# Cross attention computed transposed: row maxima turned to the keys' side, column-tiled weighing, sums inverted by ScalarE, keys and values made in the routing stage

## What is computed

```python
x = x + einsum('bsd,sod->bso', layernorm(x), ctx[itok])       # one of 32 matrices per position
x = x + routed_ffn(layernorm(x))                               # 8 experts, 256 -> 512 -> 256, gelu
q, k, v = proj(layernorm(x), Wq, bq), proj(ctx, Wk, bk), proj(ctx, Wv, bv)   # 16 heads of 16
scores = einsum('bhqd,bhkd->bhqk', q, k) / 4 + mask * -1e9
x = x + einsum('bsd,ed->bse', heads(softmax(scores) @ v), Wo) + bo
x = x + nvfp4_ffn(layernorm(x))                                # fake-quantised, 256 -> 1024 -> 256
```

## Time and profile before

| what | us |
|---|---|
| three runs | 759.76, 760.28, 765.82 |
| median | 760.28 |
| span of the profiled execution | 786.0 |
| TensorE busy in it | 611.1 (78%) |
| VectorE busy | 583.2 (74%) |
| ScalarE busy | 404.4 (51%) |
| GpSimd busy | 209.1 (27%) |

### The profile page before, as it was taken

The page is one execution under the profiler, slowest core; times in us unless marked ns, Lnnn a source line. Parts: engine busy times, 40 slices in busy tenths (PEclk is TensorE's granted clock), DMA queues, the critical chain, the costliest instruction groups (busy, mean ns, idle before and its releaser), DMA issues.

```text
span 786.0 us, 14622 instructions
## 1 busy us (share of the span) xinstructions
PE 611.1 (78%) x4239; PEld 484.1 (62%) x4240; DVE 583.2 (74%) x1515; ACT 404.4 (51%) x780; POOL 209.1 (27%) x254
## 2 busy tenths in 40 slices
PE   5496786609899999958999999999744666766766
PEld 3384655409899898847888888887611433344424
DVE  6274666855645665667888889888648999999997
ACT  1341323003434233336565667665785798778762
POOL 5617363424644565510112222211100000000000
PEclk9698797858999999978999999999975799987998
DMA  8763242259375667261000000000000000000001
GB/s 321 228 209 118 71 137 76 96 181 385 107 232 173 185 197 230 78 185 34 1 0 0 0 0 0 0 1 1 2 3 1 0 27 27 13 27 13 27 27 54
DMA packets 35230, 68.22 MB, mean 87 GB/s; under 512 B 5405, under 2 KB 24238, under 8 KB 34160
## 3 DMA queue, kind: packets, MB, share of 16 engines
q1 hardware_dynamic: 28512, 52.20, 20.2%
q0 software_dynamic: 5520, 13.61, 5.1%
q10 hardware_dynamic: 1152, 1.88, 0.8%
HBM read 53.62 MB, written 15.80 MB: 88 GB/s over the span
## 4 chain that ended last, share of the span: by engine, by line
PE 36%; DVE 19%; issue 15%; ACT 13%; DMA 7%; another core or an unknown queue 3%; SPq 3%; POOL 2%; DVEq 1%; ACTq 0%; POOLq 0%
PE bank L1289 5%; PE quad L1162 4%; PE quad L1114 4%; PE quad L1273 3%; PE bank L1304 3%; PE bank L1171 3%; ACT hqT L1013 2%; DMA x_after_ffn<-row,niU 2%; PE quad L1454 2%; PE quad L1463 2%; ACT ctxs L996 2%; PE quad L1264 2%; DVE hh L2200 2%; DMA early<-in_W 2%
## 5 line engine op out<-in xcount | busy, mean ns | idle before, releaser
L746 ACT ACTIVATE hid<-quad,early 128x128 f32<-128x128 f32 x156 | 44.5, 368 | 87.8 <-PE quad L1162 86.5
L1162 PE MATMUL quad<-xts,early 128*128 128x128 f32 x624 | 76.5, 283 | 4.5 <-DMA early<-in_W 4.3
L1162 PEld LDWEIGHTS quad<-xts,early 128*128 128x128 f32 x624 | 74.9, 199 | 6.6 <-issue 5.5
L1171 PE MATMUL bank<-W2s,hid 128*128 x312 | 70.5, 379 | 0.0
L624 POOL TENSOR_TENSOR X<-fo,X 128x256 f32<-128x256 f32 (+1 forms) x32 | 21.8, 682 | 178.0 <-DVE fo L2046 178.0
L1289 PE MATMUL bank<-nVB,nPT 128*128 128x34 f32 x512 | 63.0, 279 | 0.0
L1171 PEld LDWEIGHTS bank<-W2s,hid 128*128 128x128 f32 x312 | 57.7, 190 | 7.1
L1289 PEld LDWEIGHTS bank<-nVB,nPT 128*128 128x128 f32 x512 | 59.6, 191 | 3.7
L1489 PE MATMUL bank<-dT,hqT 128*128 128x256 bf16 x224 | 41.0, 348 | 25.8 <-ACT hqT L1013 25.7
L577 POOL DMA_INDIRECT x_after_ffn<-row,niU x39 | 39.0, 1000 | 58.9 <-DVE row L1804 41.9
L1799 DVE SCALAR_TENSOR_TENSOR row<-bank,sco,row 128x256 f32<-128x256 f32 x39 | 18.5, 474 | 47.2 <-PE bank L1171 44.3
(11 more groups left out here) (325 smaller groups left out, 1431.6 us busy)
## 6 DMA issues: line engine op xcount, KB each, us to landing
early<-in_W SPq DMA_DIRECT2D x37, 514.0 KB
row<-rows_by_expert SPq DMA_DIRECT2D x38, 134.0 KB
early<-in_ctxO SPq DMA_DIRECT2D x4, 1024.0 KB, 7.8
ctxs<-in_ctxT SPq DMA_DIRECT2D x4, 1024.0 KB
W2s<-in_W SPq DMA_DIRECT2D x8, 512.0 KB
X<-x_after_ffn SPq DMA_DIRECT2D x7, 516.0 KB, 7.2
out<-yo SPq DMA_DIRECT2D x14, 256.0 KB, 2.1
early<-in_W ACTq DMA_DIRECT2D x2, 514.0 KB
```

Of the source, the lines that this page charges most:

```text
L746: ins = act.activation(hid[:, u, c * P:(c + 1) * P], bank[2 + u][:, c * P:(c + 1) * P], ACT.Gelu, bias=W1r[:, k, DC * H2 + c:DC * H2 + c + 1])
L1162: ins = pe.matmul(bank[2 + u][:, n * P:(n + 1) * P], W1r[:, m % RING, c * H2 + n * P:c * H2 + (n + 1) * P], xt[:, u, c, :], start=c == 0, ...
L1171: ins = pe.matmul(bank[6 + u % 2][:, 0:D], hid[:, u, c * P:(c + 1) * P], W2s[:, bass.ds(ex, 1), c, :].rearrange("p o s -> p (o s)"), start ...
```

## The change

**Keys and values early.** They leave the attention. In the routing stage, behind `ranks(g-1)` of groups 1 to 8, TensorE computes keys and values of the pair g-1 straight from `ctxs`, and ScalarE copies them to `Kall` and `Vall`, which hold all pairs. Wk, Wv and bk are loaded ahead of the other weights for it, with a semaphore of their own. SP waits for VectorE's first logits (`s_dl`) before it loads the last FFN's weights.

**Scores twice.** `score` now begins with a product of ones and the mask in bf16 and adds the raw products to it in PSUM. VectorE takes only the maxima of these out (`row_max`, one instruction a half), divides them into three bf16 parts (`maxima`, four small instructions for both halves), TensorE turns them (`maxima_turn`), ScalarE copies them (`maxima_out`). `score_turned` then computes the scores with keys on partitions: a product of a selecting matrix of -1 and the maxima, and on top of it keys times queries; no probabilities are turned any more. Each of the two steps has 8 heads and all 256 queries. `exps` reads them from PSUM, with the mask of the key as its bias, and writes the probabilities in the form in which the weighing needs them. Both kinds of scores use the same four banks, in halves.

**Weighing and sums.** `weigh` has the values of two heads (32 columns) as the weight and streams 256 queries of the probabilities; four such products go to four column strips of TensorE, and four more with ones as weight give the sums, repeated on the same partitions as the values. ScalarE inverts the sums of a whole batch by a logarithm and an exponential with scale -1 (`inverse_sums`), in a table set that it loads once, VectorE multiplies (`divide`, one 128x512 instruction a batch). The result has channels on partitions, so `project` uses it without a turn. `add_rows` of VectorE adds the product straight to the residual stream, to which GpSimd has added the bias before (`biased`); GpSimd spreads the keys (`keys_in`).

**Beside these.** VectorE prepares the mask in the turned form and the selecting matrix before the FFN rows come (`key_mask`, `key_mask_rows`, some 25 instructions), and the flag also asks that the mask doesn't differ between queries. Where the narrow path ends, the scales for the next stage stand behind the last batch instead of beside the last two. Some buffers are placed anew; the weights' turns use one PSUM bank instead of two by turns.

The diff, cut to its core:

```diff
@@ SP
+            sp.dma_start(WkS[:], WkT).then_inc(s_kw, 16)
+            sp.dma_start(WvS[:], WvT).then_inc(s_kw, 16)
+            sp.dma_start(bkS[:], bk).then_inc(s_kw, 16)
...
+            sp.wait_ge(s_dl, 1)
             for n, w in enumerate((gate_w, up_w, down_w)):
@@ TensorE, routing
+            def keys_values(p):
+                if p == 0:
+                    pe.wait_ge(s_kw, 16 * 3)
+                pe.wait_ge(s_kve, p)
+                rows = [ctxs[:, 2 * p:2 * p + 2, c, S - KW:S] for c in range(DC)]
+                for n in range(DC):
+                    for c in range(DC):
+                        pe.matmul(bank[6][:, n * P:(n + 1) * P], WkS[:, c, n * P:(n + 1) * P], rows[c], start=c == 0, stop=c == DC - 1)
+                for h in range(2):
+                    for c in range(DC):
+                        ins = pe.matmul(bank[6][KW * h:KW * h + KW, D:2 * D], ctxs[:, 2 * p + h, c, S - KW:S],
+                                        WvS[:, c, :].rearrange("p (h w) -> p h w", w=VW)[:, :, 0:HD], start=c == 0, stop=c == DC - 1)
+                ins.then_inc(s_kv, 1)
...
                 if g:
                     ranks(g - 1)
+                if 0 < g <= NB // 2:
+                    keys_values(g - 1)
@@ TensorE, attention: score
+                    for k, w in enumerate(tiles):
+                        pe.matmul(scored[:, k, :], onesb[w, :], maskb[w, :], start=True, stop=False)
@@
+                def score_turned(b, h, c):
+                    if c == 0:
+                        pe.wait_ge(n_mTe, b + 1)
+                        pe.wait_ge(n_rd, b * 2 + 2)
+                    else:
+                        pe.wait_ge(n_exp, b * 2 + 1)
+                    for k, w in enumerate(tiles):
+                        pe.matmul(keyed[:, k, :], selb[w, c * P:(c + 1) * P], nMT[w, :], start=True, stop=False)
+                    for k, w in enumerate(tiles):
+                        ins = pe.matmul(keyed[:, k, :], nKB[h][w, c, :], nQT[h][w, c, :], start=False, stop=True)
+                    ins.then_inc(n_ST, 1)
+
+                def weigh(b, h, c, first=False):
+                    pe.wait_ge(n_exp, b * 2 + (c + 1))
...
+                    for k, w in enumerate(tiles):
+                        pe.matmul(duo[w, c, 0:S], nVB[h][:, 4 * c + k, :], nPT[c][:, k, :], start=True, stop=True)
+                    for k, w in enumerate(tiles):
+                        ins = pe.matmul(duo[w, c, S:2 * S], sumb[:], nPT[c][:, k, :], start=True, stop=True)
+                    ins.then_inc(n_W, 1)
@@ its order
+                def batch(b, h, first=False, stage=0):
+                    score_turned(b, h, 0)
                     if not first:
                         project(b - 1, 1)
+                    score_turned(b, h, 1)
+                    weigh(b, h, 0, first)
+                    if stage == 0:
+                        rows_in(b + 2)
...
+                    if stage < 2:
                         score(b + 1, 1 - h, 0)
+                    weigh(b, h, 1, first)
+                    if stage == 0:
+                        queries(b + 2, 0)
...
+                    if stage < 2:
+                        score(b + 1, 1 - h, 1)
+                    if stage == 0:
+                        queries(b + 2, 1)
...
+                    project(b, 0, first)
+                    if stage < 2:
+                        maxima_turn(b + 1)
@@ ScalarE
+                def exps(b, c):
+                    act.wait_ge(n_ST, b * 2 + (c + 1))
+                    act.activation(nPT[c][:], keyed, ACT.Exp, bias=keym[:, 0:1]).then_inc(n_exp, 1)
...
+                def inverse_sums(b):
+                    act.wait_ge(n_W, b * 2 + 2)
+                    act.activation(nR[:], duo[:, :, S:2 * S], ACT.Ln).then_inc(n_ln, 1)
+                    act.wait_ge(n_ln, b + 1)
+                    act.activation(nR[:], nR[:], ACT.Exp, scale=-1.0).then_inc(n_rv, 1)
@@ VectorE, its order
+                def batch(b, first=False, between=None):
+                    if not first:
+                        add_rows(b - 1, 1)
+                        new_stats(b - 1, 1)
                     if between:
                         between()
+                    row_max(b + 1, 0)
+                    row_max(b + 1, 1)
+                    divide(b)
+                    maxima(b + 1)
+                    add_rows(b, 0)
+                    new_stats(b, 0)
```

More of the change, by code:

```diff
@@ L421, in _ @@
             sp.dma_start(maskS[:], mask).then_inc(s_cw, 16)
+            for t in range(2):
+                sp.dma_start(maskC[KW * t:KW * t + KW, :], maskT[S - KW:S, :]).then_inc(s_cw, 16)
+            sp.dma_start(rowm[:, 0, :], mask[0, 0, S - KW:S].partition_broadcast(P)).then_inc(s_cw, 16)
             sp.wait_ge(s_pe0, 7)
@@ L647, in _ @@
+                pool.memset(nMb[:], 0.0).then_inc(n_z, 1)
+                for h in range(2):
+                    keys_in(0, h, h, first=True)
+                pool.wait_ge(n_fo, 1)
+                for h in range(2):
+                    biased(h)
+                for b in range(5):
+                    batch(b, b % 2, b // 2 + 1)
                 weight_first()
-                batch(5, p=4, k=1)
+                batch(5, 1, 3, k=1)
                 with pool.Fori(0, SLOTS // 2 - 1) as i:
-                    batch(i * 2 + 6, k=i * 2 + 2)
-                    batch(i * 2 + 7, p=i + 5, k=i * 2 + 3)
@@ L652, in _ @@
-                for b in range(NB - 4, NB + 1):
-                    batch(b)
+                    batch(i * 2 + 6, 0, i + 4, k=i * 2 + 2)
+                    batch(i * 2 + 7, 1, i + 4, k=i * 2 + 3)
+                for b in range(NB - 4, NB - 2):
+                    batch(b, b % 2, b // 2 + 1)
             with pool.Else():
@@ L900, in batch @@
-                    if not last and not end and b is not NB - 2:
-                        rows_out(b + 2)
-                    if p is not None:
-                        keys_out(p)
-                    if not end:
-                        exps(b, 1)
+                    if stage < 2:
+                        maxima_out(b + 1)
+                    if stage:
+                        weights_out(2 if stage == 1 else 5)
                 act.wait_ge(s_nm2, 1)
                 rows_norm(0)
-                act.wait_ge(n_kv, 1)
@@ L1277, in weigh, with maxima_turn @@
-                def weigh(b, h, q, first=False):
-                    pe.wait_ge(n_pTe, b * 2 + (q + 1))
+                def maxima_turn(b, first=False):
+                    pe.wait_ge(n_mp, b + 1)
+                    if not first:
+                        pe.wait_ge(n_cn, b)
+                    for q in range(2):
+                        ins = pe.transpose(bank[0].bitcast(BF16)[:, q * P:(q + 1) * P], nMb[:, q].rearrange("p k j -> p (k j)"), identb[:])
+                    ins.then_inc(n_mT, 1)
@@ L1342, in batch @@
-                    if not last and not end:
-                        score(b + 1, 1 - h, 0)
-                    if not end:
-                        weigh(b, h, 0, first=first)
+                    score_turned(b, h, 1)
+                    weigh(b, h, 0, first)
+                    if stage == 0:
+                        rows_in(b + 2)
+                    if stage == 1:
+                        pe.wait_ge(n_qe, NB)
+                    if stage:
+                        weights_in(0 if stage == 1 else 3)
```

522 lines of the change are left out of this document (224 added, 298 removed).

## The result

The changed kernel takes 758.13 us (median of 16 runs, 756.29 to 762.88), the kernel before 761.83 in the same comparison (16 runs, 756.06 to 768.50): a ratio of 0.995, 95% interval 0.9927 to 0.9972. I had forecast 763, no change. The time lies inside the range and within 1% of before, but the change moved it beyond the interval to the faster side, and the sum of +3 us has the wrong sign: about 7 us too much.

What follows compares the result with a forecast made beforehand. TensorE was taken as the bound in routing stage and attention. Keys and values +15, start and end with the shorter batches -14, clock +2 make +3 us on 760.28: 763 us, range 746 to 786.

Steps and rivals of the forecast that it cites:

- Keys and values early: Routing stage: a pair adds 2.55 us of TensorE to each of eight groups; +15 us in all (bounds 0 and +20).
- The rival that routing hides the keys: Routing stage: GpSimd's 10.3 us a group and creeping hide the pairs; 0 to 4 us instead of +15; chance 0.20.
- The attention: Attention batches: one chain round three engines takes 11.45 us a batch against 12.85 (bounds 10.9 and 12.1).
- TensorE late: Attention chain: TensorE reaches the second raw score 0.41 us late and the first 0.30 us late.
- The weighing: Attention: 16 records on four column strips run beside each other, 0.86 us a weighing (upper bound 3.4).
- TensorE's sum: Attention: TensorE's work in a batch falls to about 7.8 us, so no engine is the bound.
- Start and end: Attention's first scores and tail after the last batch: the FFN starts at 559.0 instead of 573.06, -14 us.
- More than two: Sign of being wrong: more than two ScalarE table loads, where one before the batches and one behind were expected.
- Key-mask preparation: Before the first rows: some 5.4 us of VectorE work hides in its 7.04 us wait; 0, +1 at most.
- The clock: Attention: a few batch stretches at TensorE's lower level, +2 us (bounds 0 and 25); as rival 784 us, chance 0.22.

Runs made afterwards that it cites:

- before_1: The kernel before, unchanged, profiled a second time: span 757.3 us.
- half_later: The kernel after with ScalarE's weight-quantisation step moved behind its copy of the turned maxima: 754.45 us, ratio 0.9886 to before.
- maxima_first: The kernel after with VectorE's maxima instructions ahead of the division, their turn ahead of the projection, and projections moved: 759.02 us, ratio 0.9949 to before.
- the disturbed profile: First profile of the unchanged kernel before, with creeping stretches in the routing stage: span 786.0 us.
- before_2: The kernel before, unchanged, profiled a third time: span 765.5 us.
- both: The kernel after with the keys-and-values pairs behind the last routing group and the maxima ahead of the division: 752.12 us, ratio 0.9856 to before.
- sums_by_dve: The kernel after with a batch's sums inverted by VectorE's reciprocal instead of ScalarE's logarithm and exponential: 841.51 us, ratio 1.1033 to before.

## Why the prediction was wrong, step by step

**Keys and values early: the step that failed.** The forecast put "+15 (bounds 0 and +20)", from 2.55 us a group of which seven should show (17.9), less part of "some 5 us" that GpSimd might swallow. A pair takes 2.09 us, and the stage grew by 6.4. The other profiles agree: four with the pairs in the stage, after among them, end it at 145.1 to 146.7 us, six without them at 138.2 to 139.7. The sentence that "as TensorE paces this stage, seven of the eight show in full" is what fails. Two other engines paced it from group 4 on: VectorE with a round of 9.75 us, and GpSimd with one of 10.3 that I had worked out from the earlier trace rows and then used for a correction only. After against before_1 shows it by first pieces: from group 1 to group 3 they are 21.4 us apart instead of 17.3, so 2.06 a group and the pair in full; from group 3 to group 9 64.1 instead of 60.0, so 0.7 a group and a third of it. Behind the last group 1.4 us were regained. The pace of 8.7 came from two groups in which TensorE was still ahead of the others, and a stretch in which it is busy for all of 10 us lay in just these groups; VectorE's 8.60 of 10 us stand in the same row, and with its idle steps inside a round it was all but full. The rival that routing hides the keys (0 to 4 us) had the mechanism, with GpSimd alone for its reason, and half of the size. This term alone is 8.6 us off, more than the whole miss.

**The attention: right.** I had 11.45 us a batch and -14 for the stage; measured are 11.42 in batches without weights' steps and -13.2. One batch in the timeline of the kernel after, the steps of the chain and the weighing:

```profile
383.75 0.29 PE L1290 MATMUL quad<-nMT,jslot 32*128 32x256 bf16 x4 [0.54 <-ACT nMT L862]
...
384.55 1.11 ACT L866 ACTIVATE nPT<-quad,keym 128x1024 f32<-128x1024 f32 x1 [0.93 <-PE quad L1292]
...
385.71 0.29 PE L1290 MATMUL quad<-nMT,jslot 32*128 32x256 bf16 x4 [0.17 <-ACT nPT L866]
...
386.37 0.16 PEld L1303 LDWEIGHTS duo<-nPT,nVB 128*32 128x32 f32 x8 [0.33 <-issue]
...
386.51 1.12 ACT L866 ACTIVATE nPT<-quad,keym 128x1024 f32<-128x1024 f32 x1
...
386.83 0.61 PE L1305 MATMUL duo<-nPT,sumb 128*32 128x256 f32 x8
...
387.37 0.42 PEld L1242 LDWEIGHTS bank<-ident,xn 128*128 128x128 f32 x4 [0.41 <-issue]
...
387.96 0.29 PE L1266 MATMUL quad<-before,onesb 32*128 32x256 bf16 x4
...
388.77 1.22 DVE L2060 TENSOR_REDUCE nM<-quad 128x16 f32<-128x1024 f32 x1 [2.20 <-PE quad L1269]
...
389.63 1.13 PE L1249 MATMUL bank<-xt,WqS 128*128 128x256 f32 x4
...
390.69 0.29 PE L1266 MATMUL quad<-before,onesb 32*128 32x256 bf16 x4
...
391.51 1.22 DVE L2060 TENSOR_REDUCE nM<-quad 128x16 f32<-128x1024 f32 x1 [1.51 <-PE quad L1269]
392.65 0.68 DVE L2074 TENSOR_TENSOR nC<-duo,nR 128x512 f32<-128x512 f32 x1
...
393.38 1.13 PE L1316 MATMUL bank<-WoS,nC 128*128 128x256 f32 x4 [0.89 <-DVE nC L2074]
...
393.89 0.19 DVE L2070 TENSOR_TENSOR nMb<-nMr,nMb 128x32 bf16<-128x32 f32 x1
...
394.35 0.28 PE L1279 MATMUL duo<-identb,nMb 128*128 128x128 bf16 x2
...
394.66 0.37 ACT L862 COPY nMT<-duo 128x256 bf16<-128x256 bf16 x1 [3.12 <-PE duo L1279]
...
395.17 0.29 PE L1290 MATMUL quad<-nMT,jslot 32*128 32x256 bf16 x4 [0.55 <-ACT nMT L862]
```

By the steps of the forecast: raw score to maximum 0.81 and 0.82 (I had 0.93); the two maxima 1.22 each (1.21); TensorE late 0.33 at the first score (0.30) and 0.70 at the second (0.41); division to projection 0.65 (0.74); to the turn 0.97 (0.95); turn and copy 0.82 (0.78); turned scores to exponential 0.80 twice (0.89); exponentials 1.16 to the next turned score and 1.12 by themselves (1.11 each). These are 11.42 in sum; the single errors are up to 0.3 us and cancel, so that the sum is this near is luck in part.

The weighing ran on four strips side by side: 16 records from 386.37 to 387.37, 1.0 us (I had 0.86, upper bound 3.4). TensorE's sum was wrong, 9.8 us a batch against 7.8. Part of it is the change of mode: the queries' four records take 1.06 us to the next start (389.63 to 390.69) where a product in the other mode follows, and such records 0.87 in the earlier trace rows, where none does. The timeline shows it as idle time of the weight loads too: 0.33 us ahead of the weighing, 0.41 ahead of the rows' turn. I had read 0.1 from the earlier trace rows. By the Trainium skill (TensorEngine Tiling (Array Packing), Key Properties) a change of tiling mode drains TensorE; here the trace agrees, with these numbers. Of it the chain has the second score's lateness, 0.70 instead of 0.41, and hardly more: none of the other terms above is more than 0.05 us over the forecast.

What I did not have is the batches with weights, 11.7 to 12.0 us. By half_later the 0.5 us are GpSimd's step beside the small instructions: "at most 0.26 each" was the bound, and they took 0.39 and 0.66. In the rows of maxima_first above GpSimd's two instructions (1.06 and 0.72 us in the mean) end near 440.74 and at 441.41, and VectorE's two at 440.77 and 441.46. The Trainium skill (SBUF — State Buffer, Who interferes with whom) has VectorE and GpSimd share a pair of ports as an exclusive lock, also for a VectorE instruction with two SBUF inputs against a GpSimd instruction that reads SBUF. The trace agrees in that each of VectorE's two instructions ends 0.03 to 0.05 us behind the one of GpSimd beside it, as if it had waited for its end.

**Start and end: right.** ScalarE's table loads stand at 333.88, 522.76 and 534.62, one before the batches and none between exponential and logarithm. More than two were named as a sign of being wrong, but the third belongs to the next stage, and before has it too, at 570.60; the first turned score comes 19.6 us after the flag (I had 19.8), and the next stage's first turn 19.7 after the last exponential (517.55 to 537.26; I had 15.4 and 4.1, and the terms listed for the 15.4 add up to 15.75).

**Key-mask preparation: right in sum, not in its reason.** The forecast hid 5.4 us of work in a wait of 7.04 us, but that wait is the disturbed profile's; in before_1 and before_2 it is 2.33 and 2.56. VectorE is busy with the new work until the first sorted rows are normalised, 10.1 us after the last scatter instead of 7.4 and 7.6; yet the flag comes no later (171.7 against 173.0 and 172.7). What absorbs the 2.6 us was not tested, so the term of nothing came true without its reason.

**The clock: right in the attention, open behind it.** No batch of the changed kernel but the first and the last fell to the lower level, and its longest holes between them are 0.89 us where the forecast had 1.4. But the quantised FFN, whose instructions did not change, took 214.8 to 219.3 us in the nine profiles with the new attention, at a granted clock of 0.80 to 0.85, and 212.9, 213.0, 219.3 and 212.9 in those with the old, at 0.83 and 0.84. If that is a rule, the change gives back some 3 us there; what decides it is not settled.

## What to carry over

Before a product is hidden or shown in a stage, count what each engine issues in one round of it, its idle steps between instructions included. An engine that is busy for three quarters of the time can be the full one (GpSimd for 77%, VectorE for 84% of the 48.6 us), and two groups at the start of a pipeline have a pace that later ones don't. Work of an engine that isn't the bound costs only what goes beyond the round of the one that is, and it is free where its own engine waits anyway: the same eight pairs cost 6.4 us in the stage and nothing behind it. A chain round three engines can be summed from single rows to a few per cent, but look at what other engines run beside its small instructions.

## What was not expected of the hardware

- Small VectorE instructions (128x32) took 0.39 and 0.66 us beside GpSimd's multiplication, and up to 0.95, where alone they take 0.17 to 0.19.
- In one of the thirteen profiles of this study three engines crept for tens of microseconds while GpSimd issued indirect DMAs at its usual pace; the routing stage took 24 us longer. No other execution showed it, and its cause stays open.
- Holes of 0.89 us ahead of the projection left TensorE's granted clock at 1.00 in the kernel after. Behind holes of 1.42 to 1.57 us it fell to the lower level in seven batches of ten (maxima_first and both), and with 4.28 us in every batch it was 0.78 (sums_by_dve).
